# Five norms in a fused transformer tower: sums of squares in four rows of 74 tokens a quarter, taken in step with the means

## What is computed

```
h = _L0_tok_ref(x, ...)
h = h + _L0_attn_ref(_layernorm(h, axis=-1), ...)
h = h + _L0_ffn_ref(_layernorm(h, axis=-1), ...)
h = h + _L1_attn_ref(_layernorm(h, axis=-1), ...)
h = h + _L1_ffn_ref(_layernorm(h, axis=-1), ...)
```

```
def _layernorm(x, axis=-1, eps=1e-05):
    m = jnp.mean(x, axis=axis, keepdims=True)
    v = jnp.var(x, axis=axis, keepdims=True)
    return (x - m) / jnp.sqrt(v + eps)

def _rmsnorm(x, w):
    return x * jax.lax.rsqrt(jnp.mean(x * x, axis=-1, keepdims=True) + _EPS) * w
```

## Time and profile before

| | |
|---|---|
| median of 3 runs | 882.53 us (880.73 to 883.51) |
| profiled execution | 881.1 us, of which the program's span 879.4 |
| TensorE busy | 793.7 us, 90% of the span |
| TensorE weight loads | 586.2 us, 67% |
| VectorE, ScalarE, GpSimd busy | 614.7, 391.3 and 183.5 us |
| mean granted TensorE clock | 0.977 of full speed |

### The profile page before, as it was taken

The page is one execution under the profiler, slowest core; times in us unless marked ns, Lnnn a source line. Parts: engine busy times, 40 slices in busy tenths (PEclk is TensorE's granted clock), DMA queues, the critical chain, the costliest instruction groups (busy, mean ns, idle before and its releaser), DMA issues.

```text
span 879.4 us, 19821 instructions
## 1 busy us (share of the span) xinstructions
PE 793.7 (90%) x7700; PEld 586.2 (67%) x7700; DVE 614.7 (70%) x976; ACT 391.3 (45%) x561; POOL 183.5 (21%) x197
## 2 busy tenths in 40 slices
PE   4998978989986988977798998799999999999997
PEld 3665757944543666755487885477777777777775
DVE  5796697678787386898767977767777655545544
ACT  5344764610224143666457965334444432323332
POOL 7000790006999801000402420000000000000000
PEclk9999979999999999999999999799999999999999
DMA  8000000020000000010130001144444322222221
GB/s 310 1 2 1 3 1 3 3 96 1 0 0 1 0 2 1 1 39 1 37 78 14 22 21 38 57 127 158 154 150 154 109 68 57 70 69 69 68 61 51
DMA packets 24073, 46.07 MB, mean 52 GB/s; under 512 B 2605, under 2 KB 10541, under 8 KB 23629
## 3 DMA queue, kind: packets, MB, share of 16 engines
q1 hardware_dynamic: 24013, 45.21, 16.8%
HBM read 41.91 MB, written 1.36 MB: 49 GB/s over the span
## 4 chain that ended last, share of the span: by engine, by line
PE 70%; DVE 21%; ACT 4%; issue 3%; POOL 1%; DMA 1%; SPq 0%; DVEq 0%; ACTq 0%; POOLq 0%
PE psum L1790 11%; PE psum L1791 11%; PE psum L1792 11%; PE psum L1982 6%; PE psum L1992 4%; PE psum L828 4%; PE psum L829 4%; PE psum L830 4%; PE psum L2124 1%; DVE arena L1460 1%; PE psum L2170 1%; DVE arena L1658 1%; PE psum L1963 1%; PE psum L2187 1%; PE psum L2156 1%
## 5 line engine op out<-in xcount | busy, mean ns | idle before, releaser
L1790 PE MATMUL psum<-xh,arena 128*128 128x296 f16 (+1 forms) x664 | 193.3, 291 | 8.3 <-DVE xl L1333 5.0
L1791 PE MATMUL psum<-xl,arena 128*128 128x296 f16 (+1 forms) x664 | 193.2, 291 | 0.0
L1792 PE MATMUL psum<-xh,arena 128*128 128x296 f16 (+1 forms) x664 | 193.2, 291 | 0.0
L697 DVE TENSOR_TENSOR arena<-arena 128x592 f16<-128x592 f32 x68 | 52.7, 775 | 61.1 <-ACT arena L608 60.8
L603 ACT ACTIVATE arena<-psum 128x592 f32<-128x592 f32 x66 | 43.8, 664 | 115.7 <-PE psum L1792 115.7
L1790 PEld LDWEIGHTS psum<-xh,arena 128*128 (+2 forms) x664 | 65.3, 98 | 30.8 <-DVE xl L1333 4.5
L752 DVE TENSOR_TENSOR arena<-psum,arena 128x592 f32<-128x592 f32 x64 | 49.6, 775 | 50.8 <-PE psum L1792 50.6
L828 PE MATMUL psum<-arena 128*128 128x296 f16 x272 | 79.9, 294 | 4.6 <-DVE arena L697 3.8
L608 ACT ACTIVATE arena<-arena 128x592 f16<-128x592 f32 x66 | 46.0, 696 | 77.6 <-DVE arena L691 74.8
L829 PE MATMUL psum<-arena 128*128 128x296 f16 x272 | 79.9, 294 | 0.0
L830 PE MATMUL psum<-arena 128*128 128x296 f16 x272 | 79.8, 293 | 0.0
(11 more groups left out here) (321 smaller groups left out, 1675.3 us busy)
## 6 DMA issues: line engine op xcount, KB each, us to landing
arena<-comb SPq DMA_DIRECT2D x62, 296.0 KB, 3.3
arena<-in_wmoe SPq DMA_DIRECT2D x34, 384.0 KB, 3.0
arena<-in_xt SPq DMA_DIRECT2D x4, 864.0 KB, 9.6
arena<-in_w SPq DMA_DIRECT2D x2, 1024.0 KB, 6.6
arena<-arena SPq DMA_DIRECT2D x6, 187.0 KB
arena<-in_ctrl SPq DMA_DIRECT2D x1, 1056.0 KB, 9.1
out<-arena SPq DMA_DIRECT2D x2, 512.0 KB, 3.1
arena<-in_wlin SPq DMA_DIRECT2D x1, 768.0 KB, 4.4
```

Source lines behind the costliest of these rows:

```text
L697: dve.tensor_tensor(al[:, s_], t1, ah[:, s_], ALU.subtract).then_inc(ev["al"], 1)
L1790: pe.matmul(dst, wh, mh, start=start, stop=False)
L1791: pe.matmul(dst, wh, ml, start=False, stop=False)
L1792: return pe.matmul(dst, wl, mh, start=False, stop=stop)
```

## The change

A quarter of 296 tokens is cut into `PARTS = 4` parts of `PART = 74`. Its sums of squares no longer stand as 32 equal rows of 296, but in rows 32q to 32q + 3, 74 tokens in each. The weights `mean_comb` are 35 columns, zero but for column 3; the window of 32 columns that starts at 3 - x puts the sum in row x and adds zero to the other 31. Square root and reciprocal then work on 128 x 74. `spread_parts` picks row x out with a column of the identity, broadcast to 128 weight columns, one matmul for each part.

In ln1, ln2 and ln4 the sums of quarter x - 1 now follow the mean of quarter x; only the last quarter's sums stand behind the loop. ln3 keeps its order, and so does cn. `KEEP["rec"]` goes from 16 to 9 for all five.

```
-KEEP = {"rec": 16, ...
+KEEP = {"rec": 9, ...
+        mean_comb = sb("mean_comb", [128, 32 + PARTS - 1])
...
+            link(pool.memset(mean_comb[:], 0.0))
+            link(pool.memset(mean_comb[:, PARTS - 1:PARTS], 1.0 / D))
...
-                act.activation(sd, bank((name, "v"))[:, 0:CH], ACT.Sqrt, bias=eps[:, 0:1]).then_inc(emptied["act"], 1)
+                act.activation(sd[:, 0:PART], bank((name, "v"))[:, 0:PART], ACT.Sqrt, bias=eps[:, 0:1]).then_inc(emptied["act"], 1)
...
-                dve.reciprocal(sd, sd).then_inc(ev[name + "_rec"], 1)
+                dve.reciprocal(sd[:, 0:PART], sd[:, 0:PART]).then_inc(ev[name + "_rec"], 1)
...
+            def part_sums(bk, q, squared):
+                for x in range(PARTS):
+                    for c, src in enumerate(squared):
+                        ins = pe.matmul(bk[32 * q:32 * q + 32, 0:PART], mean_comb[:, PARTS - 1 - x:PARTS - 1 - x + 32],
+                                        src[:, PART * x:PART * x + PART], start=x + c == 0,
+                                        stop=x == PARTS - 1 and c == len(squared) - 1)
+                return ins
+
+            def spread_parts(ps, q, roots):
+                rows = slice(32 * q, 32 * q + 32)
+                for x in range(PARTS):
+                    ins = pe.matmul(ps[:, PART * x:PART * x + PART],
+                                    ident[rows, 32 * q + x:32 * q + x + 1].to_broadcast([32, 128]),
+                                    roots[rows, 0:PART], start=True, stop=True)
+                return ins
...
+                def sums(q):
+                    pe.wait_ge(ev[name + "_sq"], q + 1)
+                    return part_sums(fill((name, "v")), q, [sq[:, c, cols(q)] for c in range(2)])
...
+                        if x and name != "ln3":
+                            sums(x - 1)
-                bk = fill((name, "v"))
-                for q in range(NCH):
-                    pe.wait_ge(ev[name + "_sq"], q + 1)
-                    ps = bk[32 * q:32 * q + 32, 0:CH]
-                    pe.matmul(ps, mean_ones[:, 0:32], sq[:, 0, cols(q)], start=True, stop=False)
-                    ins = pe.matmul(ps, mean_ones[:, 0:32], sq[:, 1, cols(q)], start=False, stop=True)
+                for q in range(0 if name == "ln3" else NCH - 1, NCH):
+                    ins = sums(q)
...
-                    rows = slice(32 * q, 32 * q + 32)
-                    pe.matmul(fill((name, "r", q))[:, 0:CH], spread[rows], sd[rows], start=True, stop=True).then_inc(filled[who((name, "r", q))], 1)
+                    spread_parts(fill((name, "r", q)), q, sd).then_inc(filled[who((name, "r", q))], 1)
```

More of the change, by code:

```diff
@@ L20 @@
 CH = BC * S
+PARTS = 4
+PART = CH // PARTS
 HG, HJ = 4, 4
@@ L206 @@
 FILLERS = 5
-KEEP = {"rec": 16, "mx1": 18, "tok": 12, "xq": 12, "mx2": 20, "hq": 12, "split": 12, "combine": 12, "op": 14, "csq": 36,
+KEEP = {"rec": 9, "mx1": 18, "tok": 12, "xq": 12, "mx2": 20, "hq": 12, "split": 12, "combine": 12, "op": 14, "csq": 36,
         "qkrec": 32, "km": 30, "on": 24}
@@ L1102, in _ @@
             full(act, ("cv",))
-            act.activation(r3[:, 0:CH], bank(("cv",))[:, 0:CH], ACT.Sqrt, scale=D / BW, bias=eps[:, 1:2]).then_inc(emptied["act"], 1)
+            act.activation(r3[:, 0:PART], bank(("cv",))[:, 0:PART], ACT.Sqrt, scale=D / BW, bias=eps[:, 1:2]).then_inc(emptied["act"], 1)
             for q in range(NCH):
@@ L1433, in _ @@
             after(dve, ("cv",))
-            dve.reciprocal(r3[:, 0:CH], r3[:, 0:CH]).then_inc(ev["crec"], 1)
+            dve.reciprocal(r3[:, 0:PART], r3[:, 0:PART]).then_inc(ev["crec"], 1)
             for q in range(NCH + 1):
@@ L1890, in _ @@
                 pe.wait_ge(ev["csq"], q // 2 + 1)
-                ins = pe.matmul(bk[32 * q:32 * q + 32, 0:CH], mean_ones[:, 0:32], rp[:, cols(q)], start=True, stop=True)
+                ins = part_sums(bk, q, [rp[:, cols(q)]])
             ins.then_inc(filled[who(("cv",))], 1)
@@ L1895, in _ @@
             for q in range(NCH):
-                rows = slice(32 * q, 32 * q + 32)
-                pe.matmul(fill(("cr", q))[:, 0:CH], spread[rows], r3[rows, 0:CH], start=True, stop=True).then_inc(filled[who(("cr", q))], 1)
+                spread_parts(fill(("cr", q)), q, r3).then_inc(filled[who(("cr", q))], 1)
             pe.wait_ge(ev["dwl"], 1)
```

## The result

| | before | changed |
|---|---|---|
| median of 19 runs each | 882.89 us | 886.22 us |
| all runs | 879.79 to 886.53 | 882.04 to 888.44 |
| ratio (95% interval) | | 1.0033 (1.0018 to 1.0048) |
| profiled execution, span | 881.1, 879.4 | 887.8, 886.1 |
| TensorE busy, matmul rows | 793.7, 7700 | 811.2, 8001 |

The change costs 3.3 us. Three executions that took far longer (1166 us once in the third experiment, 2027 and 2771 us for the kernel before beside four of the experiments) are left out of every comparison.

A forecast was written before the change was run, and what follows sets the result against it. A dense matmul stream on TensorE (90% busy) that stands still for VectorE, five times at norms; -6.0 us at the norms + 6.8 for sums in step = +0.8, forecast 883.3 us, range 876.5 to 889.5.

The forecast's parts named there:

- A: Leading case: the gain at the reciprocals is given back by sums moved onto a full TensorE; 880.5 to 886 us, 50%.
- Square root and reciprocal: In all five norms, 74 columns instead of 296: reciprocal 0.62 us, square root 0.35, together 1.55 us gained a norm.
- Spreading: Reciprocals spread over 128 partitions in eight short passes a quarter, 0.11 us each: first bank full 0.35 us later.
- All four still run side by side: In the spread, the four quarters use four row groups and were taken to keep running in parallel, as before.
- rival C: Quarters no longer run side by side if TensorE's look-ahead is under fifteen passes: 7.6 us on top of A, 890.9 us; 20%.
- Net gain a norm: Narrow square root and reciprocal less the later spread: 1.55 - 0.35 = 1.2 us a norm, 6.0 us over five norms.
- I cost these at nothing: Sums of squares in short passes: same time for the last quarter; cn's side-by-side quarters and ln3's kept order add 0 us.
- In step: Sums of quarters 0 and 1 moved between the means: 2.44 us lost in ln1 and ln2, 1.9 in ln4, 6.8 together.
- 1.6 lost: Rival C's term in ln1: a serial spread with mask products behind it delays the first product by 1.6 us.
- Masks: Nine mask products in each wait end within 0.1 us of the reciprocal: no gain; sixteen would run 0.9 us too long.
- Rival D: Fewer mask products and short passes bring two or three more stretches at 1.2 GHz: 3 to 5 us more, about 887; 8%.
- rival B: Sums in step with the means are free, so only the 6.0 us gain is left: 876.5 us; 22%.

The follow-up runs named there:

- the third experiment: Changed kernel with sums back behind the means, and both the sums' and the spread's matmuls written in turn across quarters: 876.57 us, ratio 0.9932.
- the runs of the spread: Spread's matmuls written in turn: with late sums also in turn 876.57 us, as the only edit to the changed kernel 888.70 us.
- the first experiment: Changed kernel with all sums of squares back behind the last mean in ln1, ln2 and ln4, still in 74-column parts: 882.39 us, ratio 0.9987.

## Why the prediction was right, and where not

The forecast was 883.3 us, and 886.22 was measured: +3.3 against +0.8 us. That is inside the range of 876.5 to 889.5, which was held wide for the rivals, and 0.2 us above the 886 that A alone was given; at 0.33% it is just past the 0.3% that was called no change. The main terms and their signs were right. The missing 2.5 us are ln3 (forecast -1.2, measured +0.26), cn (0.4 less gained), the blocks in step (0.4) and the spread's first bank (0.3 in ln1, ln2 and ln4). They add up to 2.6 in the traces, and part of ln3's is the clock, so that the close match with the medians is luck.

- **Square root and reciprocal**: 0.616 and 0.324 us against 0.62 and 0.35. Right.
- **Spreading**, first bank: 0.35 later was forecast. From the end of the reciprocal (42.80 + 0.62) to the scaling at 44.68 are 1.26 us, against 0.86 before: 0.40. In the other four norms it is 1.33, so 0.47. The pace of 0.11 was right. "All four still run side by side" was wrong: 2.63 us. It didn't matter, as the runs of the spread show. The sign named for rival C, passes of quarter 3 that end over 2 us after the reciprocal, did appear (46.17 against 43.42, 2.75).
- **Net gain a norm**: 1.2 forecast, 1.14, 1.07 and 1.05 measured in ln1, ln2 and ln4, 0.80 in cn. In cn the sums of two quarters run 0.99 us instead of 0.69, since the second waits for the first; "I cost these at nothing" failed there by 0.3.
- **ln3, the step that failed.** "ln3 keeps its order. I cost these at nothing" was wrong by 1.3 us: four times sixteen passes shut one another out, and the low clock lay on ten of them. The serial order is 0.74 of it, as ln2 and ln4 of the first experiment show at full clock; the ten slow passes are the other 0.6. Rival C had this term for the right reason, but at 1.4 nearly twice its size.
- **In step**: 2.44, 2.44 and 1.9 forecast, 2.60, 2.60 and 2.01 measured, and 6.5 together by the median of the run that has only this (2.53, 2.53 and 1.96 in its trace). Right, each by 0.1 to 0.2 too small: a block costs 1.24 and the mean behind it starts its second pass late.
- **Rival C** was true as a mechanism and far oversized as a price. The look-ahead is three waiting passes in a group, less than the fifteen it decided on; it cost 0.74 in ln3 and 0.3 in cn, not 7.6. The step that failed in it is "1.6 lost" behind the spread: it took the first product for the stage, where VectorE's pace decides from the second quarter on, and it took the passes for wholly serial.
- **Two rules.** The Trainium skill says that matmuls keep the program's order in their starts and ends (TensorE: Matmul & The Clock Gate, Part 3). These runs show otherwise for matmuls of different column or row groups: their starts leave the program's order as long as no group has more than three passes waiting. The Trainium skill also says that a change of the tiling mode drains TensorE (TensorEngine Tiling (Array Packing), Key Properties). The 0.1 us each way in a block agree with that.
- **Masks**: they end with the reciprocal, as worked out, and sixteen would have cost 0.9 a norm.
- **Rival D**: more time at 1.2 GHz did come, 60 us for 40, with its sign, a granted clock of 0.50 in ln3's wait. It stood beside A and did not replace it: 1 to 2 of the 3.3 us by the estimate above. What brings the low stretches stays open.

With the sums back behind the means and the order of neighbours mended, the change is what it could have been: 876 to 877 us, 0.7% faster than before. That is rival B's 876.5, reached by another way: not by sums that are free in step, but by taking them out of step.

## What to carry to other kernels

Work that costs nothing because it fills a wait is not made cheaper by doing it earlier; look at whether the engine has idle time in the place where it goes. When a matmul for a 32-column or 32-row group is cut into several short ones, write the groups in turn, part by part: a group that has three passes waiting holds up every other group behind it. And count what a cut makes serial in the stages whose order did not change.

## What the runs showed of the hardware

- TensorE starts matmuls of different column or row groups out of the program's order. One running and three waiting passes to a group, with a stop at the first matmul whose group is full, gives the times of all five cases: 64 passes of 74 columns take 1.92 us from first to last start in turns of one or two matmuls, 2.71 in turns of four, and 3.4 with the quarters one after another (3.62 less the last pass's 0.23).
- An fp32 pass of 74 columns with new 32-column weights starts every 0.064 us (the sums), with new 128-column weights every 0.11 us (the spread). The transposes of the earlier trace rows, also 74 columns on 128-column weights, started every 0.069, so the width of the weights alone doesn't give the pace.
- The granted clock differs between runs of one program: 0.966 to 0.976 in 19 runs of the changed kernel, and the runs at 0.972 or more were on average 3.2 us shorter than those at 0.970 or less.
- A change between 128-column and 32-column work costs 0.1 us each way: 0.34 between starts where 0.25 is the pace, and 0.16 where it is 0.064.
